# Layer statistics of two tiles in one VectorE instruction

## The reference

```python
zn = ln(ln_c(x)); pp, lp, ip = ln(protein_pair), ln(l_pair), ln(inter_pair)     # 128 channels each
gate = lambda v, Wg, W: sigmoid(v @ Wg + bg) * (v @ W + b)                      # 128 -> 64
ab1, ab2, ab3 = (gate(zn, ...) * mask for each of three weight sets)
block = einsum('ikc,kjc->ijc', gate(pp), ab1) + einsum('ikc,jkc->ijc', ab2, gate(lp)) + ab3 * gate(ip)
x = x + sigmoid(zn @ Wend + bend) * (ln(block) @ Wsum + bsum) * mask            # ln over 64 channels
t = ln(x)                                                                       # 128 channels
y = sum over the 2 chosen experts e of w_e * (gelu(t @ W1[e] + b1[e]) @ W2[e] + b2[e])
x = x + ln(y + t) * gamma + beta                                                # 128 channels
```

## Time and profile before

| what | value |
|---|---|
| median of three runs | 1425.35 us (1424.94 to 1429.03) |
| span of the profiled execution | 1419.6 us |
| own time of the profiled execution | not given apart from the three runs; the median lies 5.75 us above the span |
| PE busy | 1344.6 us, 95% |
| DVE busy | 1216.5 us, 86%, 4125 instructions |
| ACT, POOL busy | 1001.3 us (71%), 999.5 us (70%) |
| statistics in the projection stage (L693) | 672 early and 480 late ones |

### The profile page before, as it was taken

One profiled execution on the slowest core, in us unless ns is written; L12 is line 12 of the kernel. 1 busy time (PEld: TensorE's weight loads), 2 busy tenths in 40 slices (PEclk: granted clock), 3 DMA queues, 4 the chain that ended last, 5 costly groups with the idle time before them and its releaser, 6 DMA issues. The chain is left out here.

```text
span 1419.6 us, 32205 instructions
## 1 busy us (share of the span) xinstructions
PE 1344.6 (95%) x9880; PEld 1129.9 (80%) x9880; DVE 1216.5 (86%) x4125; ACT 1001.3 (71%) x2327; POOL 999.5 (70%) x1559
## 2 busy tenths in 40 slices
PE   6999999999999997999799999699999999999994
PEld 3877788877888777999666667599999999999984
DVE  7998899989989884888799998667888888888997
ACT  3888888888888886565467776346677766776773
POOL 4999999999999996444388888334555555655574
PEclk9999999999999999999899999799999999999997
DMA  9999999999999999788699995211222232222213
GB/s 218 229 252 253 254 249 251 258 255 254 243 255 258 257 243 296 269 293 306 169 281 301 300 300 177 94 45 51 84 75 75 75 87 78 75 77 79 84 45 89
DMA packets 357530, 267.48 MB, mean 188 GB/s; under 512 B 60432, under 2 KB 332722, under 8 KB 357362
## 3 DMA queue, kind: packets, MB, share of 16 engines
q1 hardware_dynamic: 355800, 264.76, 70.0%
q10 hardware_dynamic: 1290, 0.46, 0.2%
q0 software_dynamic: 272, 0.21, 0.1%
HBM read 171.02 MB, written 94.37 MB: 187 GB/s over the span
## 5 line engine op out<-in xcount | busy, mean ns | idle before, releaser
L1558 ACT ACTIVATE hT<-psH_d,b 128x512 f32<-128x512 f32 x288 | 197.9, 689 | 154.7 <-PE psH_d L1598 154.6
L675 PE MATMUL psZ_a<-w_all,xT_a 128*128 128x128 f32 x1728 | 229.9, 276 | 0.0
L675 PE MATMUL psZ_a<-w_all,xT_block 128*128 128x384 f32 x576 | 214.0, 495 | 5.2 <-DVE low_ab L744 5.1
L675 PEld LDWEIGHTS psZ_a<-w_all,xT_a 128*128 128x128 f32 x1728 | 209.8, 192 | 2.3 <-ACT xT_a L583 2.1
L599 ACT ACTIVATE sig_a<-psZ_a 128x256 f32<-128x256 f32 (+1 forms) x360 | 153.8, 427 | 79.2 <-PE psZ_a L675 49.5
L611 POOL TENSOR_SCALAR shared<-shared,coefs_early 128x128 f32<-128x128 f32 x468 | 204.7, 460 | 0.0
L662 PE MATMUL psT_a<-ident,shared 128*128 128x128 f32 x1152 | 186.1, 274 | 3.7 <-issue 2.1
L662 PEld LDWEIGHTS psT_a<-ident,shared 128*128 128x128 f32 x1152 | 141.0, 142 | 54.9 <-issue 26.7
L1252 DVE TENSOR_SCALAR shared<-shared,coef 128x128 f32<-128x128 f32 x288 | 179.2, 681 | 1.6 <-POOL xh_b L1632 1.6
L1625 POOL TENSOR_TENSOR u_d<-u_d,gamma 128x512 f32<-128x512 f32 x72 | 94.1, 1307 | 117.4 <-ACT u_d L1541 116.0
L1632 POOL TENSOR_TENSOR xh_b<-shared,b 128x512 f32<-128x512 f32 x72 | 93.5, 1298 | 105.0 <-DVE ffn_sum L1693 103.8
(11 more groups left out here) (234 smaller groups left out, 3165.1 us busy)
## 6 DMA issues: line engine op xcount, KB each, us to landing
shared<-in_x_dram SPq DMA_DIRECT2D x48, 512.0 KB, 5.7
scratch_xT<-xT_block SPq DMA_DIRECT2D x36, 512.0 KB, 5.2
shared<-scratch_xT SPq DMA_DIRECT2D x36, 512.0 KB, 5.0
scratch_x<-x_c SPq DMA_DIRECT2D x36, 512.0 KB, 4.0
shared<-scratch_x SPq DMA_DIRECT2D x36, 512.0 KB, 3.4
shared<-in_x_dram SPq DMA_DIRECT2D x48, 256.0 KB, 5.2
shared<-L_conv_protein_pair_dram SPq DMA_DIRECT2D x24, 512.0 KB, 6.8
shared<-in_L_conv_l_pair_dram SPq DMA_DIRECT2D x24, 512.0 KB, 9.1
```

Source lines behind the costliest of these rows:

```text
L675: ins = nc.tensor.matmul(out, turned_x(G, i, t0, size)[:, j * P:j * P + P], rhs[i], start=True, stop=True)
L1558: nc.scalar.activation(hT[:, S % 2, f, :], psH[:, f, :], ACT.Gelu, bias=s["b1"][:, f:f + 1]).then_inc(gelued, 1)
```

## The change

`pair_stats` gives `bn_stats` two neighbouring tiles as one operand whose innermost index is the tile: it reads column 0 of the first, column 0 of the second, column 1 of the first, and so on, 256 columns (128 for `tri`). The two sets of three numbers that the instruction writes then belong to one tile each. So there are half as many statistics instructions in all stages, and the chains no longer add and subtract halves: their first five steps become one that divides the sum of squares and adds epsilon. The tables that place statistics and chain steps are rewritten for pairs and shorter chains. In the mixing stage the final factor goes to PSUM, and the FFN's statistics get two buffers.

```diff
 RSQRT_STEPS = 8
-LN_STEPS = 5 + RSQRT_STEPS + 1
+LN_STEPS = 1 + RSQRT_STEPS + 1
+PAIR_STATS = 3
+COUNT, MEAN, SQUARES = range(PAIR_STATS)
+
+
+def pair_stats(nc, stats, two_tiles):
+
+
+    return nc.vector.bn_stats(stats.rearrange("p t s -> p (t s)"), two_tiles.rearrange("p t c -> p c t"))
...
 FIRST_STATS = [[] for _ in range(NG_A)]
-share_out(FIRST_STATS, AT_X, 8, 2, 0, range(TPB))
-share_out(FIRST_STATS, AT_X + 3, 8, 3, 0, range(IP_SPLIT))
-share_out(STATS_A, AT_X, 5, 2, 0, range(LP_AHEAD, TPB))
-share_out(STATS_A, AT_X + 2, 4, 3, 0, range(IP_SPLIT))
-share_out(COEFS_A, AT_X + 4, 4, EARLY, 0, range(CHAIN_STEPS))
-share_out(STATS_A, AT_X + 8, 4, 3, 0, range(IP_SPLIT, TPB))
-share_out(STATS_A, AT_PP, 5, 0, 1, range(TPB))
-share_out(COEFS_A, AT_PP + 5, 4, LATE, 1, range(CHAIN_STEPS))
-share_out(STATS_A, AT_LP + 4, 5, 1, 1, range(TPB))
-share_out(STATS_A, AT_IP + 3, 5, 2, 1, range(LP_AHEAD))
+share_out(FIRST_STATS, AT_X, 4, 2, 0, range(0, TPB, 2))
+share_out(FIRST_STATS, AT_X + 3, 4, 3, 0, range(0, IP_SPLIT, 2))
+share_out(STATS_A, AT_X, 3, 2, 0, range(LP_AHEAD, TPB, 2))
+share_out(STATS_A, AT_X + 2, 2, 3, 0, range(0, IP_SPLIT, 2))
+share_out(COEFS_A, AT_X + 4, 3, EARLY, 0, range(CHAIN_STEPS))
+share_out(STATS_A, AT_X + 8, 2, 3, 0, range(IP_SPLIT, TPB, 2))
+share_out(STATS_A, AT_PP, 3, 0, 1, range(0, TPB, 2))
+share_out(COEFS_A, AT_PP + 5, 3, LATE, 1, range(CHAIN_STEPS))
+share_out(STATS_A, AT_LP + 4, 3, 1, 1, range(0, TPB, 2))
+share_out(STATS_A, AT_IP + 3, 3, 2, 1, range(0, LP_AHEAD, 2))
...
 def chain_step(nc, dve, step, stepped, before, stats, work, parts, rstd, shift, ready):
     v = nc.vector
     tiles = stats.shape[1]
-    mean2, m2, diff, sq, var, t = (work[:, q, 0:tiles] for q in range(6))
+    var, t = (work[:, q, 0:tiles] for q in range(2))
     y = rstd
     if step > 0:
         dve.wait_ge(stepped, before + step)
     if step == 0:
-        ins = v.tensor_tensor(work[:, 0:2, 0:tiles].rearrange("p q w -> p w q"), stats[:, :, 1:3], stats[:, :, 4:6], ALU.add)
-    elif step == 1:
-        ins = v.tensor_tensor(diff, stats[:, :, 1], stats[:, :, 4], ALU.subtract)
-    elif step == 2:
-        ins = v.scalar_tensor_tensor(sq, diff, 0.25, diff, ALU.mult, ALU.mult)
-    elif step == 3:
-        ins = v.scalar_tensor_tensor(var, m2, 1.0 / CH, sq, ALU.mult, ALU.add)
-    elif step == 4:
         for lo, hi, factor, addend in parts:
-            ins = v.tensor_scalar(var[:, lo:hi], var[:, lo:hi], factor, addend, ALU.mult, ALU.add)
-    elif step < 5 + RSQRT_STEPS:
-        ins = rsqrt_step(v, step - 5, y, t, var)
+            ins = v.tensor_scalar(var[:, lo:hi], stats[:, lo:hi, SQUARES], factor / CH, addend, ALU.mult, ALU.add)
+    elif step < 1 + RSQRT_STEPS:
+        ins = rsqrt_step(v, step - 1, y, t, var)
     elif step == LN_STEPS - 1:
-        ins = v.scalar_tensor_tensor(shift, mean2, -0.5, y, ALU.mult, ALU.mult)
+        ins = v.scalar_tensor_tensor(shift, stats[:, :, MEAN], -1.0, y, ALU.mult, ALU.mult)
     else:
...
-LN_STEPS_C = 15
+LN_STEPS_C = 11
 CHAIN_STEPS_C = LN_STEPS_C + 1
+NEAR_ROWS, FAR_ROWS = 2, 5
...
-    mean2, m2, var, t, e, shift = rows(far, 6)
-    diff, sq, raw, y, w = rows(near, 5)
+    var, t, e, root, shift = rows(far, FAR_ROWS)
+    y, w = rows(near, NEAR_ROWS)
     of = stats[:, lo:hi].rearrange("p k w s -> p (k w) s")
     if step > 0:
         dve.wait_ge(stepped, before + step)
     if step == 0:
-        ins = v.tensor_tensor(far[:, 0:2, lo:hi, :].rearrange("p q k w -> p (k w) q"), of[:, :, 1:3], of[:, :, 4:6], ALU.add)
+        for k in kinds:
+            ins = v.tensor_scalar(far[:, 0, k, :], stats[:, k, :, SQUARES], 1.0 / channels[k], EPS5, ALU.mult, ALU.add)
     elif step == 1:
-        ins = v.tensor_tensor(diff, of[:, :, 1], of[:, :, 4], ALU.subtract)
-    elif step == 2:
-        ins = v.scalar_tensor_tensor(sq, diff, 0.25, diff, ALU.mult, ALU.mult)
-    elif step == 3:
-        for k in kinds:
-            ins = v.scalar_tensor_tensor(near[:, 2, k, :], far[:, 1, k, :], 1.0 / channels[k], near[:, 1, k, :], ALU.mult, ALU.add)
+        ins = v.tensor_scalar(y.bitcast(I32), var.bitcast(I32), -0.5, float(RSQRT_MAGIC), ALU.mult, ALU.add)
+    elif step in (2, 5):
+        ins = v.scalar_tensor_tensor(t, y, -0.5 if step == 2 else 1.0, var, ALU.mult, ALU.mult)
+    elif step in (3, 6):
+        ins = v.tensor_tensor(e, t, y, ALU.mult)
     elif step == 4:
...
-        ins = v.scalar_tensor_tensor(y, t, 1.875, y, ALU.add, ALU.mult)
+    elif step == 9:
+        ins = v.scalar_tensor_tensor(root, t, 1.875, y, ALU.add, ALU.mult)
     else:
-        ins = v.scalar_tensor_tensor(shift, mean2, -0.5, y, ALU.mult, ALU.mult)
+        ins = v.scalar_tensor_tensor(shift, root, -1.0, of[:, :, MEAN], ALU.mult, ALU.mult)
...
-                ins = v.bn_stats(chain_stats[chain][:, at, :], tiles_in[i][:, t, :])
-                if at == (EARLY_TILES, LATE_TILES)[chain] - 1 or (n == NBLK - 1 and (i, t) == (3, TPB - 1)):
+                ins = pair_stats(nc, chain_stats[chain][:, at:at + 2, :], tiles_in[i][:, t:t + 2, :])
+                if at == (EARLY_TILES, LATE_TILES)[chain] - 2 or (n == NBLK - 1 and (i, t) == (3, TPB - 2)):
...
-                for t in (2 * j, 2 * j + 1):
-                    ins = v.bn_stats(stats_t[:, par, t, :], s["tri"][:, bass.ds(TPB * n + t, 1), :].rearrange("p o c -> p (o c)"))
+                ins = pair_stats(nc, stats_t[:, par, 2 * j:2 * j + 2, :], s["tri"][:, TPB * n + 2 * j:TPB * n + 2 * j + 2, :])
...
-                    v.scalar_tensor_tensor(coef_t[:, par, 1, :], far[:, 5, TRI_KIND, :], 1.0, zm, ALU.add, ALU.mult).then_inc(coefst_ready, 1)
-                    v.tensor_tensor(coef_t[:, par, 0, :], near[:, 3, TRI_KIND, :], zm, ALU.mult).then_inc(coefst_ready, 1)
+                    v.scalar_tensor_tensor(coef_t[:, par, 1, :], far[:, 4, TRI_KIND, :], 1.0, zm, ALU.add, ALU.mult).then_inc(coefst_ready, 1)
+                    v.tensor_tensor(coef_t[:, par, 0, :], far[:, 3, TRI_KIND, :], zm, ALU.mult).then_inc(coefst_ready, 1)
                 if x2_there:
                     now = s["coef_2"][:, :, bass.ds(TPB * (n - 2), TPB)]
-                    v.tensor_copy(now[:, 1, :], far[:, 5, X2_KIND, :]).then_inc(coefs2_ready, 1)
-                    v.tensor_copy(now[:, 0, :], near[:, 3, X2_KIND, :]).then_inc(coefs2_ready, 1)
+                    v.tensor_copy(now[:, 1, :], far[:, 4, X2_KIND, :]).then_inc(coefs2_ready, 1)
+                    v.tensor_copy(now[:, 0, :], far[:, 3, X2_KIND, :]).then_inc(coefs2_ready, 1)
...
-    FIRST_STEPS_C[6 + _step // 7].append(_step)
+    FIRST_STEPS_C[6 + _step // 6].append(_step)
...
-CHAIN_SPLIT = 7
+CHAIN_SPLIT = 5
...
-        stats, work, coef = sb("stats_d", [P, TPB, 6]), sb("work_d", [P, 6, TPB]), sb("coef_d", [P, 2, 2, TPB])
+        stats, work, coef = sb("stats_d", [P, 2, TPB, PAIR_STATS]), sb("work_d", [P, 2, TPB]), sb("coef_d", [P, 2, 2, TPB])
...
-                ins = v.bn_stats(stats[:, 4 * g + i, :], vv[:, par, 4 * g + i, :])
-                if i == 3:
+                t = 4 * g + i
+                ins = pair_stats(nc, stats[:, par, t:t + 2, :], vv[:, par, t:t + 2, :])
+                if i == 2:
                     ins.then_inc(statted, 1)
```

More of the change, by code:

```diff
@@ L105, in rsqrt_step, with ln_step @@
     return v.scalar_tensor_tensor(y, t, 1.875, y, ALU.add, ALU.mult)
-def ln_step(nc, dve, step, stepped, before, stats, work, channels, mulv, addv, rstd, shift, plus=0.0):
+def ln_step(nc, dve, step, stepped, before, stats, work, channels, addv, rstd, shift):
     v = nc.vector
-    mean2, m2, diff, sq, var, t = (work[:, k, :] for k in range(6))
+    var, t = (work[:, k, :] for k in range(2))
     y = rstd
@@ L155, in ln_pair_step @@
     if step == 0:
[L156 removed]
+        for k in kinds:
+            ins = v.tensor_scalar(far[:, 0, k, :], stats[:, k, :, SQUARES], 1.0 / channels[k], EPS5, ALU.mult, ALU.add)
     elif step == 1:
[L158 to L171 removed]
+        ins = v.tensor_scalar(y.bitcast(I32), var.bitcast(I32), -0.5, float(RSQRT_MAGIC), ALU.mult, ALU.add)
[3 more added lines that the diff above has]
+        ins = v.tensor_tensor(e, t, y, ALU.mult)
+    elif step == 4:
+        ins = v.scalar_tensor_tensor(y, e, 1.5, y, ALU.add, ALU.mult)
+    elif step == 7:
+        ins = v.tensor_scalar(w, e, 0.375, -1.25, ALU.mult, ALU.add)
     elif step == 8:
[L173 to L176, removed]
         ins = v.tensor_tensor(t, e, w, ALU.mult)
[L178 to L179 removed]
+    elif step == 9:
+        ins = v.scalar_tensor_tensor(root, t, 1.875, y, ALU.add, ALU.mult)
     else:
[L181 removed]
+        ins = v.scalar_tensor_tensor(shift, root, -1.0, of[:, :, MEAN], ALU.mult, ALU.mult)
     ins.then_inc(stepped, 1)
@@ L754, in body @@
                             v.tensor_tensor(prod, z, gate, ALU.mult).then_inc(multiplied, 1)
-            for t in range(CHUNKS[1][1]):
+            for t in range(0, CHUNKS[1][1], 2):
                 stats_of(0, 0, t)
             setup_vector_first(dve)
-            for t in range(*CHUNKS[2]):
```

(16 more changed lines are left out.)

17 lines of the change are left out of this document (3 added, 14 removed).

## The result

The changed kernel takes **1398.47 us** (median of four runs, 1397.42 to 1400.89) against 1425.14 us before (four runs, 1422.93 to 1429.03): a ratio of 0.982, 95% interval 0.9807 to 0.9831, 26.7 us faster. The full-pace rival (1403 us, chance 0.30) had the right sign and the right price of the instruction.

What follows compares the result with a forecast made beforehand. PE was taken to bound the projection and FFN stages, DVE the mixing stage. Projection +48, mixing +15, FFN 0 and ends +1.5 made +64.5 us, giving 1490 us; 8-in-10 range 1402 to 1550.

Steps and rivals of the forecast that it cites:

- full-pace rival: All statistics: alternating read at one column a cycle, -0.06 us a pair; total 1403 us, chance 0.30.
- What bounds the kernel: PE paces projection and FFN stages; DVE paces mixing at 1.33 us a slot, with PE next at 1.23.
- The price of the alternating read: Paired statistics: 2.0 ns a column, so a pair of 128 tiles adds 0.57 us in place of 0.39.
- first form (a line of each tile is held): Reason for the full-pace rival: in paired statistics a buffer may hold a line of each tile.
- second (a limit on stepped accesses in total): Other reason for the full-pace rival: the limit applies to the engine's stepped accesses in total; a 384-column copy ran at 0.95 ns.
- half pace: Main case for paired statistics: alternating reads run at about half pace, losing time in projection; 1490 us, chance 0.55.
- From a price to a time: Working from pair price to kernel time: ten groups of 2.04 us against 1.30, bursts partly hidden, +4.0 us a projection block.
- Chains: Norm chains lose four steps: -3.6 us a projection block (2.27 early, 1.34 late), -1.2 us a mixing block.
- Projection stage: Dearer pairs outrun PE's cover in full groups: +4.0 us a block, +48 us over 12 blocks.
- Mixing stage: Net +0.14 us on each of 132 slots, 18 us, less about 3 from idle time: +15 us.
- FFN stage: Two pairs a slot add 0.36 us, covered by PE with 1.0 us a slot: 0.
- Ends: Start +2.8 us; chains standing alone -0.85 each, against +0.7 and +0.36 for pairs ahead: together +1.5.

Runs made afterwards that it cites:

- experiment 2: Changed kernel with isolated 240-column statistics ahead of the mixing stage, varying tiles in turn and step; two tiles in turn took 0.41 us, four 0.57.
- Experiments 1 and 2: the probe and experiment 2: both add isolated instructions to the changed kernel ahead of the mixing stage; no whole-kernel time is given.
- the probe: Changed kernel with isolated DVE and ACT statistics, copies and additions ahead of the mixing stage; stepped 256-column statistics took 0.59 to 0.62 us, against 0.43 contiguous.
- read_twice: Changed kernel with each pair read twice within its statistics instruction, doubling the columns; 1492.88 us, ratio 1.048.
- mixing_old: Changed kernel with single-tile statistics, the four removed chain steps and the old tables back in the mixing stage alone; 1412.23 us, ratio 0.9919.

## Why the prediction was wrong

**What bounds the kernel** was read rightly: PE in the projection stage, DVE in the mixing stage with PE at 1.23 us a slot behind it. The slots came out at 1.23.

**The price of the alternating read is the step that failed.** The forecast had "a stepped stream runs at about half the pace, 1.84 to 2.38 ns a column. I take 2.0": a pair of 128 tiles adding 0.57 us. It adds 0.335. The nearest rows were chosen by the wrong likeness. A read with a step and a read of two tiles in turn are both not contiguous, but by the simplest reading of experiment 2 the first takes one element of each line and the second takes all of them, in an order that leaves two lines open. Experiments 1 and 2 part the two: steps of 16 bytes and more cost 1.8 ns a column, two tiles in turn 1.08. Even for stepped statistics 2.0 was high: it lay between ACT's 1.84, which is ACT's own pace (its contiguous copies have 0.83), and the addition's 2.38. The factor of 1.7 for DVE's copies, read from a cast of 256 columns and a copy on 64 partitions, was right: the probe has (0.51 - 0.139)/(0.36 - 0.139) = 1.7.

The Trainium skill, SBUF — State Buffer, section "Door 1: The DMA port swizzle", has lines of 16 bytes and two hits in a line for full bandwidth. By that rule the trace agrees for steps: 0.41 us at 8 bytes, 0.58 at 16. Its other half, that each access which crosses to a new line pays, does not hold here. In the alternating read every access crosses, and it costs nothing (0.41 against 0.41); the measurement decides.

**The rival's reason** fits in its first form (a line of each tile is held), as far as two tiles go, and is wrong in its second (a limit on stepped accesses in total): one stepped stream alone slows statistics to 1.8/1.08 = 1.7 times. Its total of 1403 is in part luck: it had 4.4 us too much gain in the projection stage and 7.1 too little in the FFN stage and at the ends.

**Rows that might have told.** DVE's addition into every 64th element has a stepped read and a stepped write. The forecast took its 2.38 ns as the price of a stepped stream; in the probe one stepped operand costs 0.12 us on 192 columns and two, a read and a write, cost no more (0.48 both; two stepped reads 0.52). The kernel's addition, whose other operand lies in PSUM, takes 0.579 us for as many columns; what makes the difference no run shows. In the trace of before no row has one operand that takes two contiguous streams in turn, so the rival could not be excluded, nor could the forecast be reached without choosing. With the chance for full pace at 0.30 the row for "half pace" was held too firmly; an even split would have been what those rows bear.

**From a price to a time** was nearly right, and read_twice shows it: 1492.9 us where this way gives about 1500 for its price, with blocks, slots and FFN stage close to where the forecast had them.

**Chains.** The forecast took 3.6 us a block from the projection chains, 2.27 early and 1.34 late. By the rows of the same view of after, twelve early chains lost 0.70 us of instructions each and four gaps of 0.035, 0.84 together; the late one 1.87 and gaps, 2.0. Together 2.9. The new step 0 "at the same cost" as the old fifth step (0.175 us) lasts 0.75, and three other steps that took 0.22 us each now take 0.62 to 0.66. The timeline of one early chain of after, with POOL beside DVE, shows why:

```profile
75.41 0.83 POOL L615 TENSOR_TENSOR sig_a<-sig_a,mask 128x384 f32<-128x384 f32 x1
75.52 0.78 DVE L348 TENSOR_SCALAR work_a<-stats_early 128x56 f32<-128x56 f32 x1
...
76.91 0.83 POOL L615 TENSOR_TENSOR sig_a<-sig_a,mask 128x384 f32<-128x384 f32 x1 [0.24 <-ACT sig_a L582]
77.16 0.66 DVE L106 SCALAR_TENSOR_TENSOR work_a<-work_a 128x56 f32<-128x56 f32 x1
...
78.43 0.83 POOL L615 TENSOR_TENSOR sig_a<-sig_a,mask 128x384 f32<-128x384 f32 x1 [0.20 <-ACT sig_a L582]
78.70 0.63 DVE L110 SCALAR_TENSOR_TENSOR work_a<-work_a 128x56 f32<-128x56 f32 x1
```

Each long step starts while POOL's masking product runs and ends 0.06 to 0.08 us after it (76.24 and 76.30, 77.74 and 77.82, 79.26 and 79.33). Which step is long is set by where it falls, one in nearly every group, and taking steps away moves the collision to another. The old 0.730 was of this kind too (in the same place of the trace of before the step ends at 78.76 and POOL's product at 78.69), and in part the old 0.874, whose step ends 0.22 us behind (77.41 and 77.19). That this is what holds them is read from the times alone; no run took POOL's product away.

**Projection stage.** Forecast +48 us, measured -2.6; the rival had -7, all of PE's idle time. Of that idle time DVE held only a part: with 114 us less work on it the stage shrinks by 4.2 us more.

**Mixing stage.** Forecast +15, the rival -13, measured -12.8, and 13.8 by mixing_old. The reason given for it in the rival was right: PE sets a slot. In its last block nothing changed, two slots still take 2.46 us with DVE waiting for PE:

```profile
854.46 0.42 DVE L1204 TENSOR_TENSOR y_c<-psW_c,end_gate 128x256 f32<-128x256 f32 x1 [0.71 <-PE psW_c L1127]
...
856.92 0.42 DVE L1204 TENSOR_TENSOR y_c<-psW_c,end_gate 128x256 f32<-128x256 f32 x1 [0.71 <-PE psW_c L1127]
```

**FFN stage.** Forecast 0 in both cases, measured -4.7, of which 3.3 lie in the last 89 us. The cover of 1.0 us a slot was a mean over 72 slots. In the last 89 us (13 slots) DVE was busy 81.3, so it had 0.6 us a slot, and in two of them it was late all the same. The other 1.4 us are not settled.

**Ends.** Forecast +1.5 (its terms add up to 1.3), the rival -2.5; measured -0.6 at the start, -1.6 and -1.6 at the two chains that stand alone, -1.1 at the end, -4.9 in all. At the head of the mixing stage the twelve pairs take 2.44 us where 24 single tiles took 3.14, -0.7, and the chain alone from its first to its last step 0.9 us less (3.46 and 2.55). Both terms follow from the rival's prices, which give some -4.2 in all (28 pairs at -0.06 and three chains at -0.85); its -2.5 was added up too low.

## What to carry to other kernels

Where the trace has no row for an access pattern, ask which bytes stay unused between its accesses and how many streams it takes in turn, not only whether the pattern is contiguous, and let two unlike nearest rows share the chance evenly. A short instruction's duration beside another engine may be that engine's; before costing its removal, see whether it ends when something else ends. A stage's mean slack says nothing of its last blocks: read their window by itself.

## What the hardware showed that was not expected

- Statistics of two tiles read in turn cost what contiguous ones do: 0.41 us for 240 columns, with the tiles 512 bytes or 4 KB apart; three tiles 0.44, four 0.57.
- A step of 8 bytes is free, one of 16 bytes takes 0.58 us for the same 240 columns.
- On an addition of 192 columns a stepped read and a stepped write together cost no more than either alone (0.48 us against 0.36 without); two stepped reads take 0.52.
- Statistics and gating products keep their durations beside POOL's masking product (0.75 us for two pairs at 74.29 and again at 81.44), while short chain steps of 56 columns stretch from 0.19 or 0.22 us to 0.62 to 0.78 and end just behind it.
